# Squares of the queries: a 32-bit product replaced by high and low parts that GpSimd splits

## The reference, cut to what matters

```python
def rms_norm(x, scale, eps=EPS):
    ms = jnp.mean(jnp.square(x), axis=-1, keepdims=True)
    return x * jax.lax.rsqrt(ms + eps) * scale
...
q = rms_norm(x @ q_w + q_b, nq_s).reshape(B, S, H, D)
k_txt = rms_norm(txt_ctx @ k_w + k_b, nkt_s).reshape(B, -1, H, D)
...
out_txt = sdpa(q, k_txt, v_txt)
```

## Time and profile before

| what | value |
|---|---|
| three runs | 1923.73, 1924.05, 1924.66 us; median 1924.05 us |
| the profiled execution: its own time | 1923.51 us |
| its span, first to last instruction | 1921.7 us |
| mean granted TensorE clock | 0.972 |
| PE, PEld, DVE, ACT, POOL busy in the span | 91%, 80%, 73%, 51%, 60% |
| stretch from 60 to 240 us, most of it `project` | PE busy 19.4 to 19.7 us of each 20 us |

### The profile page before, as it was taken

How to read it: one execution, slowest core, us unless ns; L and a number is a source line. 1 busy time by engine, 2 the same in 40 slices (tenths; PEclk the granted TensorE clock), 3 DMA queues, 4 the chain that set the end, 5 groups by cost and what they waited for, 6 DMA issues and landing times. The chain is left out here.

```text
span 1921.7 us, 30704 instructions
## 1 busy us (share of the span) xinstructions
PE 1757.4 (91%) x8735; PEld 1537.2 (80%) x8735; DVE 1400.8 (73%) x2586; ACT 985.4 (51%) x1659; POOL 1147.9 (60%) x987
## 2 busy tenths in 40 slices
PE   7899979999999999999999999999992998699998
PEld 6566669888888888888898898888892887588887
DVE  4344477977978878878878879788772565577777
ACT  3354445555655655655555556556552553244443
POOL 1000178888788788788888887887862331133333
PEclk8999989999999999999999999999996999699999
DMA  3365564465554665554554565556535782133332
GB/s 109 106 214 205 193 174 111 110 120 117 122 121 112 129 128 117 122 131 115 115 134 108 115 127 125 116 115 130 101 89 187 249 275 86 64 117 108 121 108 80
DMA packets 417360, 251.19 MB, mean 131 GB/s; under 512 B 350267, under 2 KB 368827, under 8 KB 415516
## 3 DMA queue, kind: packets, MB, share of 16 engines
q1 hardware_dynamic: 417308, 250.55, 50.9%
HBM read 187.71 MB, written 60.10 MB: 129 GB/s over the span
## 5 line engine op out<-in xcount | busy, mean ns | idle before, releaser
L1322 ACT ACTIVATE p_high<-psum,key_rms 128x448 fp32r<-128x448 f32 x384 | 244.9, 638 | 396.9 <-PE psum L1145 396.8
L1143 PE MATMUL psum<-p_high,c_high 128*128 128x448 f32 (+1 forms) x768 | 287.9, 375 | 47.8 <-DVE p_low L1405 47.8
L1405 DVE TENSOR_TENSOR p_low<-psum,p_high 128x448 fp32r<-128x448 f32 x384 | 236.4, 616 | 99.8 <-ACT psum L1324 98.6
L1143 PE MATMUL psum<-u_high,c_high 128*128 128x448 f32 x768 | 286.0, 372 | 20.3 <-DVE psum L1416 14.0
L1144 PE MATMUL psum<-u_low,c_high 128*128 128x448 f32 x768 | 282.8, 368 | 0.0
L1145 PE MATMUL psum<-u_high,c_low 128*128 128x448 f32 x768 | 281.8, 367 | 0.0
L1145 PE MATMUL psum<-p_high,c_low 128*128 128x448 f32 (+1 forms) x768 | 281.4, 366 | 0.0
L1144 PE MATMUL psum<-p_low,c_high 128*128 128x448 f32 (+1 forms) x768 | 281.0, 366 | 0.0
L1416 DVE COPY psum<-beta_wide 128x448 f32<-128x448 f32 x416 | 259.4, 627 | 20.5 <-DMA beta_wide<-absorbed_biases 4.7
L1617 POOL TENSOR_TENSOR c_low<-stage,c_high 128x512 fp32r<-128x512 f32 x208 | 274.0, 1317 | 0.0
L1324 ACT ACTIVATE psum<-psum,key_rms 128x448 f32<-128x448 f32 x384 | 232.5, 606 | 0.0
(11 more groups left out here) (246 smaller groups left out, 4026.8 us busy)
## 6 DMA issues: line engine op xcount, KB each, us to landing
stage<-in_ctx SPq DMA_DIRECT2D x210, 256.0 KB, 2.8
averages<-o_raw SPq DMA_DIRECT2D x64, 448.0 KB, 5.2
o_stage<-averages SPq DMA_DIRECT2D x32, 896.0 KB, 5.6
u_raw<-absorbed_queries SPq DMA_DIRECT2D x60, 448.0 KB, 5.6
absorbed_queries<-u_stage SPq DMA_DIRECT2D x14, 1792.0 KB, 6.8
beta_wide<-absorbed_biases SPq DMA_DIRECT2D x32, 448.0 KB, 5.0
recip_wide<-reciprocals SPq DMA_DIRECT2D x32, 448.0 KB, 4.0
p_wide<-probs_by_expert SPq DMA_DIRECT2D x32, 448.0 KB, 3.6
```

Source lines behind the costliest of these rows:

```text
L1143: nc.tensor.matmul(out, high, rhigh, start=start, stop=False, **kw)
L1322: nc.scalar.activation(p_high[:, probs_slot(u), :], src, ACT.Exp, scale=key_rms[:, t:t + 1])
L1405: return nc.vector.tensor_tensor(out, a, b, ALU.subtract)
```

## The change

The squares are still made by ScalarE in 32 bits. GpSimd then makes for each half `square_high` (a copy to F32R) and `square_low` (the square less its high part), and TensorE multiplies each of them by `square_w`, which is F32R now: two F32R passes for each half in place of one 32-bit matmul. `q_square`, `square_high` and `square_low` have room for one head, and so there are new waits: ScalarE writes the high query and the square of a half of head h only when GpSimd has split that half of head h - 1; GpSimd writes a half only when TensorE has summed that half of the head before; TensorE's squares wait for GpSimd's split in place of ScalarE's square. `first_tiles[5]` on GpSimd now stands behind the last split.

```diff
-        q_square = sb("q_square", [P, 2, N])
+        q_square = sb("q_square", [P, N])
+        square_high, square_low = sb("square_high", [P, N], F32R), sb("square_low", [P, N], F32R)
...
             def squares(h):
                 for half in range(2):
-                    pe.wait_ge(q_taken, 2 * h + half + 1)
-                    nc.tensor.matmul(psum[0:ROWS_SQ, SUMS + half, 0:HALF], square_w[:, h, :],
-                                     q_square[:, h % 2, cols(half)], start=h == 0, stop=h == H - 1)\
-                        .then_inc(squares_summed, 1)
+                    pe.wait_ge(square_split, 2 * h + half + 1)
+                    out = psum[0:ROWS_SQ, SUMS + half, 0:HALF]
+                    nc.tensor.matmul(out, square_w[:, h, :], square_high[:, cols(half)], start=h == 0, stop=False)
+                    nc.tensor.matmul(out, square_w[:, h, :], square_low[:, cols(half)], start=False,
+                                     stop=h == H - 1).then_inc(squares_summed, 1)
...
-                if h >= 2:
-                    act.wait_ge(squares_summed, 2 * (h - 1))
                 for half in range(2):
                     unit = ("q", h, half)
+                    if h >= 1:
+                        act.wait_ge(square_split, 2 * (h - 1) + half + 1)
                     act.wait_ge(q_done, done(unit))
                     src = psum[:, bank[unit], 0:HALF]
                     nc.scalar.activation(q_high[:, h % QRING, cols(half)], src, ACT.Identity, bias=bias)
-                    nc.scalar.activation(q_square[:, h % 2, cols(half)], src, ACT.Square, bias=bias)\
+                    nc.scalar.activation(q_square[:, cols(half)], src, ACT.Square, bias=bias)\
                         .then_inc(q_taken, 1)
...
         def gpsimd(gp):
-            first_tiles[5](gp)
+            for h in range(H):
+                for half in range(2):
+                    n = 2 * h + half
+                    square, high = q_square[:, cols(half)], square_high[:, cols(half)]
+                    gp.wait_ge(q_taken, n + 1)
+                    if h >= 1:
+                        gp.wait_ge(squares_summed, n - 1)
+                    nc.gpsimd.tensor_copy(high, square).then_inc(square_high_ready, 1)
+                    gp.wait_ge(square_high_ready, n + 1)
+                    nc.gpsimd.tensor_tensor(square_low[:, cols(half)], square, high.bitcast(F32), ALU.subtract)\
+                        .then_inc(square_split, 1)
+                if h == H - 1:
+                    first_tiles[5](gp)
```

More of the change, by code:

```diff
@@ L224, in build @@
                 bias_low = sb("bias_low", [P, BIAS_FLAT], F32R, proj)
-                square_w = sb("square_w", [P, H, 1 + 2 * H], stack=proj)
+                square_w = sb("square_w", [P, H, 1 + 2 * H], F32R, proj)
                 begun = prologue(nc, xT_in, kwb_in, small_in, psum, xT, ident, ones, minus_half, zeros, small, key_scale,
@@ L294, in _ @@
                 nc.gpsimd.memset(part[:, :].bitcast(F32), 0.0).then_inc(zeros_ready, 1)
-            nc.gpsimd.memset(square_w[:, :, :], 0.0).then_inc(square_w_zero, 1)
+            nc.gpsimd.memset(square_w[:, :, :].bitcast(F32), 0.0).then_inc(square_w_zero, 1)
             gp.wait_ge(ident_ready, 1)
@@ L445, in project @@
             sem("q_done"), sem("q_taken"), sem("q_split"), sem("squares_summed"))
+        square_high_ready, square_split = sem("square_high_ready"), sem("square_split")
         u_done, u_act, u_dve, biases_done = sem("u_done"), sem("u_act"), sem("u_dve"), sem("biases_done")
```

## The result

| | before | after |
|---|---|---|
| median (runs) | 1924.05 us (5) | 1931.07 us (5) |
| lowest and highest | 1920.56, 1925.53 us | 1926.11, 1932.44 us |
| ratio of the times | | 1.0031, 95% interval 1.002 to 1.0042 |
| the profiled execution, its span | 1923.51, 1921.7 us | 1926.11, 1924.3 us |
| mean granted clock in it | 0.972 | 0.971 |

The changed kernel is slower, by 0.31%, more than the 0.2% that was forecast as no change (the interval starts just there), and inside the range. The execution that was profiled is the fastest of its five; the other four took 1930.4 to 1932.4 us. What makes them longer had to be found in further traces.

A forecast was written before the change was run, and what follows sets the result against it. The prediction took TensorE to bound the projection. Shorter squares (-12.9 us), VectorE's delay reaching TensorE (+15.4) and a small allowance (+0.3) made +2.8 us: 1926.9 us, +0.15%, counted as no change, range 1914 to 1933.

The forecast's parts named there:

- The saving of a head: TensorE's squares in each head: short F32R passes take 1.23 us in place of 2.15, saving 0.92 us.
- Heads 0 and 1: Ahead of the loop, GpSimd's four splits delay the squares: nothing saved or lost, 0.3 us more allowed.
- The hold: In each loop head, GpSimd's SBUF reads block VectorE's `wk_low`, so the copies of u start 1.1 us later.
- My doubt about the copy: No row showed GpSimd's copy holding a VectorE operation; if it holds nothing, the delay is 0.96 us, not 1.1.
- TensorE feels it all: TensorE's pass waiting for VectorE's first copy of u has no slack: 14 x 1.1 = 15.4 us added.
- The sum: Whole kernel: -12.9 + 15.4 + 0.3 = +2.8 us, giving 1926.9 us, +0.15%, no change that counts.
- 14 x 0.92: Squares of heads 2 to 15 in the loop: TensorE's saving counted for all 14, 12.9 us off.
- The inner range: Whole kernel's time for delays of 0.96 to 1.26 us a head: 1924.5 to 1930 us.
- the clock falls: Rival: TensorE's longer wait in a head brings 1.2 GHz, 6.9 us a head hit, 1934 us or more; chance 0.03.

The follow-up runs named there:

- b_short: The kernel before with squares written as F32R and two F32R passes over them for each half, low part left out, GpSimd idle: 1910.26 us, ratio 0.9931.
- a_wait: The changed kernel with GpSimd's second split of a head put behind VectorE's `wk_low` and `wq_low` by two waits: 1913.24 us, ratio 0.9944.
- b_pool: The kernel before, 32-bit squares kept, with GpSimd making high and low parts of the squares that nobody reads: 1940.80 us, ratio 1.0082.
- b_copy: The kernel before, 32-bit squares kept, with GpSimd making two unread copies for each half, no subtraction: 1927.20 us in one execution.
- a_order: The changed kernel with the weights' high and low parts made ahead of the query's own, on ScalarE and VectorE: 1906.65 us, ratio 0.9904.
- a_again: The changed kernel, unedited, run again: 1930.57 us, ratio 1.0033 against the kernel before.
- b_set: The kernel before, 32-bit squares kept, with GpSimd doing two memsets for each half, which write SBUF and read nothing: 1925.04 us in one execution.

## Why the prediction was nearly right, point by point

- **The saving of a head.** 0.92 predicted, 0.94 in the changed trace; alone (b_short) 0.94 as well. Right.
- **Heads 0 and 1.** Biases of head 1 were to start at 70.4; they start at 70.16, in a trace whose first square (61.96) is 0.26 early against the earlier trace rows. Right: no gain, no loss.
- **The hold.** Predicted: first `wk_low` held by the second copy, second by the second subtraction, `wq_low` free, ends 0.29 behind GpSimd's. So it came, with 0.28; the two took 0.61 and 1.37 us, where I had 0.7 and 1.4; the delay 1.09 to 1.15, taken as 1.1, measured 1.07, while a head took 11.51 and not 11.55. a_wait and b_pool show it from both sides. My doubt about the copy was settled by b_copy. GpSimd's subtraction took 1.15 us in the median of a_wait and 1.16 in that of a_order, where `wk_low` doesn't meet it, near the 1.13 of the earlier trace rows, and not the 0.98 estimated from the Trainium skill ("GPSIMD Engine Reference", Elementwise — side-by-side cycle accounting).
- **TensorE feels it all.** Right: 1.34 us at the one place.
- **The sum.** +2.8 us predicted. With the clock at full it is 2.1 + 1.0 = 3.1 us. But the saving was counted 14 times. The step that failed there is "14 x 0.92": the 14th, that of head 15, is spent in the wait for `square_sums`. All kernels with short squares wait at the same place for the same 1.1 us. The inner range, "1924.5 to 1930", is wider than its own delays give: 0.96 and 1.26 make 1924.9 and 1929.1.
- **The clock.** This is what made the kernel slower and not the same. I gave "the clock falls" 0.03, since a wait of 1.32 us between busy stretches had left it up. In the loop such a wait recurs every 11.5 us and now and then the clock falls, 0, 1 and 2 times in three traces; behind the loop it falls in two of the three. The price was off too: I had a whole head of 42 passes at the lower level, 6.9 us; the level was low for 3.4 us and a fall cost 1.5. Averaged over its 14 runs (`after` and a_again) the changed kernel takes 1930.0 us, and the kernel before 1923.9 over the 23 runs beside the experiments: 6.1 us. Of these 3.1 are the terms of full clock; a fall of 1.6 behind the loop in two traces of three makes 1.1, and one fall in the loop, the mean of the three, 1.5. That is an estimate of 5.7 from few traces, and 0.4 stay open.

So the mechanism named first was right and the sum at full clock within 0.3 us, though it was +2.8 us against the 6 to 7 measured: half of the loss came from a rival that I held unlikely.

## What to carry to other kernels

Work put on an idle GpSimd is not free for VectorE: where GpSimd reads SBUF while VectorE has an operation with two inputs there, they take turns, each whole operation at a time, and if VectorE is what TensorE waits for, a head pays more (1.07 us) than a good change gives (0.94). Look in the timeline for what VectorE does in that very microsecond and move one of them: moving two lines, on each of two engines, turned +0.3% into -0.96%, of which 0.39 are the new order by itself. And a saving on TensorE counts only as often as TensorE is what ends last: check the last turn of the loop by itself.

## What the runs showed of the hardware

- A held VectorE operation of 256 columns ended 0.28 us behind GpSimd's operation, whatever that was, a copy of 0.56 us or a subtraction of 1.21; a memset of 0.47 us and a `wq_low` of 0.41 inside it did not slow each other (b_set, one meeting).
- Of two VectorE operations in a row, the first and the second can each be held: GpSimd, waiting, gets in between (110.61 to 112.51 in the changed kernel).
- The granted clock fell to 1.2 GHz behind waits of only 1.1 to 1.3 us, in an otherwise busy stretch, and not behind all of them: three times in 42 such waits in the loop of the changed kernel, four times in 14 in b_pool, and never in the loops of the ten traces without such a wait.
